# A fused convolution, attention and expert kernel: the group 1/sqrt of the convolution seeded by a GpSimd power

## The reference, cut to what matters

```python
def _gn(v, G=32, eps=1e-05):
    B_, H_, W_, C_ = v.shape
    g = v.reshape(B_, H_, W_, G, C_ // G)
    m = jnp.mean(g, axis=(1, 2, 4), keepdims=True)
    s = jnp.var(g, axis=(1, 2, 4), keepdims=True)
    return ((g - m) / jnp.sqrt(s + eps)).reshape(v.shape)

x = x + _L0_conv_ref(_gn(x), L0_conv_W1, L0_conv_b1)
```

## Time and profile before

| what | value |
| --- | --- |
| three runs | 760.74, 761.24, 767.37 us; median 761.24 |
| the profiled execution | 759.72 us |
| its span, first to last instruction | 757.9 us |
| granted TensorE clock, mean over the span | 0.974 of full speed |
| busy over the span | PE 91%, PEld 82%, DVE 61%, ACT 44%, POOL 34% |

### The profile page before, as it was taken

One profiled execution on the slowest core, in us unless ns is written; L12 is line 12 of the kernel. 1 busy time (PEld: TensorE's weight loads), 2 busy tenths in 40 slices (PEclk: granted clock), 3 DMA queues, 4 the chain that ended last, 5 costly groups with the idle time before them and its releaser, 6 DMA issues.

```text
span 757.9 us, 16610 instructions
## 1 busy us (share of the span) xinstructions
PE 691.6 (91%) x4136; PEld 619.3 (82%) x4137; DVE 465.8 (61%) x1718; ACT 335.1 (44%) x500; POOL 259.9 (34%) x250
## 2 busy tenths in 40 slices
PE   3987886899999999994799999999999999999993
PEld 3876776788878788882699999998999998999893
DVE  5788988667777787777445454454545444454541
ACT  2433334566666667561343443433344343333330
POOL 3544554105343443434232232322223232322322
PEclk9999999999999999997799999999999999999997
DMA  8211111002121211112622222222222222222221
GB/s 270 87 47 47 31 49 42 12 11 80 47 73 52 68 57 44 72 43 89 179 36 37 42 31 42 36 37 36 37 41 32 42 36 37 36 37 41 32 31 16
DMA packets 32570, 40.08 MB, mean 53 GB/s; under 512 B 4853, under 2 KB 27990, under 8 KB 32424
## 3 DMA queue, kind: packets, MB, share of 16 engines
q1 hardware_dynamic: 18566, 25.98, 12.0%
q0 software_dynamic: 13296, 13.35, 11.6%
q10 hardware_dynamic: 690, 0.55, 0.3%
HBM read 22.38 MB, written 17.47 MB: 53 GB/s over the span
## 4 chain that ended last, share of the span: by engine, by line
DMA 33%; issue 10%; DVE 5%; PE 1%; SPq 1%; DVEq 1%; POOLq 0%; POOL 0%; ACT 0%
DMA out_rows<-y_sb,y_id 32%; DVE y_sb L1017 3%; DVE y_id L1014 1%; PE ps L1034 1%; DVE y_sb L1012 1%; DMA slot_rows<-lists 1%; DVEq L1012 1%; SPq L424 0%; POOLq L606 0%; DVEq L1017 0%; SPq L425 0%; SPq L486 0%; POOL out_rows L603 0%; SPq L487 0%; SPq L497 0%
## 5 line engine op out<-in xcount | busy, mean ns | idle before, releaser
L603 POOL DMA_INDIRECT out_rows<-y_sb,y_id x71 | 110.8, 1560 | 273.4 <-DVE y_sb L1017 260.0
L1034 PE MATMUL ps<-w_o_sb,hT 128*128 x852 | 158.2, 336 | 10.1 <-DVE hT L1022 6.1
L1034 PEld LDWEIGHTS ps<-w_o_sb,hT 128*128 128x128 f32 x852 | 137.7, 191 | 26.8 <-issue 26.8
L700 ACT ACTIVATE h_sb<-ps 128x768 f32<-128x768 f32 x71 | 57.5, 810 | 224.0 <-PE ps L1034 224.0
L1012 DVE TENSOR_TENSOR y_sb<-ps,b_o_sb 128x192 f32<-128x192 f32 x71 | 25.4, 358 | 170.8 <-DMA out_rows<-y_sb,y_id 165.2
L1034 PE MATMUL ps<-w_hi,sT_hi 96*128 (+1 forms) x284 | 103.8, 365 | 1.3 <-DVE sT_lo L1000 1.3
L1034 PE MATMUL ps<-w_hi,sT_lo 96*128 (+1 forms) x284 | 97.5, 343 | 0.0
L1034 PE MATMUL ps<-w_lo,sT_hi 96*128 (+1 forms) x284 | 97.0, 342 | 0.0
L700 ACT ACT_TABLE_LOAD x71 | 91.1, 1283 | 6.4 <-issue 5.1
L1022 DVE COPY hT<-ps 128x384 f32<-128x384 f32 x142 | 72.1, 550 | 1.4 <-PE ps L1236 1.4
L1236 PE MATMUL ps<-const,h_sb 128*128 128x128 f32 x426 | 58.2, 273 | 1.9 <-ACT h_sb L700 1.9
(11 more groups left out here) (192 smaller groups left out, 1308.8 us busy)
## 6 DMA issues: line engine op xcount, KB each, us to landing
slot_rows<-lists SPq DMA_DIRECT2D x71, 97.0 KB, 2.1
w_o_sb<-in_w_o SPq DMA_DIRECT2D x8, 576.0 KB
out_rows<-w_o_sb SPq DMA_DIRECT2D x16, 192.0 KB, 1.8
h_sb<-in_split_w SPq DMA_DIRECT2D x9, 288.0 KB
hT<-in_split_w SPq DMA_DIRECT2D x9, 288.0 KB
w_o_sb<-in_x SPq DMA_DIRECT2D x1, 1536.0 KB, 12.3
out_rows<-y_sb,y_id POOLq DMA_INDIRECT x71, 3.5
w_o_sb<-in_x SPq DMA_DIRECT2D x1, 768.0 KB, 9.0
```

Of the source, the lines that this page charges most:

```text
L603: pool.indirect_dma_start(out=out, out_offset=bass.IndirectOffsetOnAxis(ap=y_id[:, 0:1], axis=0), in_=y_sb[:, :], in_offset=None, compute_ ...
L700: act.activation(h_sb[:, :].rearrange("p (b n) -> p b n", b=2), ps_h, ACT.Gelu).then_inc(h_done, 1)
L1034: return pe.matmul(dst, lhsT, rhs, start=start, stop=stop)
```

## The change

The seed no longer comes from bit arithmetic on DVE but from a power on GpSimd, gvar to the -0.5, with a tile of constants -0.5 as its second operand. One Newton round is left of three. GpSimd's order in a step becomes xc, power, w_lo, xn. DVE's order in the middle of the step becomes: gneg, gvar, both bn_stats, gsum reduction, first multiply (it waits for the power), bn_aggr, second multiply, copy of the moments, grs, gsq reduction. So the gsq reduction stands behind grs, where it stood ahead of the third round before.

```diff
+        minus_half = sb("minus_half", [P, GROUPS])
+        gpow = sb("gpow", [P, GROUPS])
...
+        gvar_done, gpow_done = sem("gvar_done"), sem("gpow_done")
...
+                         (minus_half[:, :], -0.5))
...
+                if not absent(i + 2):
+
+                    wait(pool, grs_done, i + 2)
+                    wait_alone(pool, gvar_done, i + 3, ld_const)
+                    pool.tensor_tensor(gpow[:, :], gvar[:, :], minus_half[:, :], ALU.pow).then_inc(gpow_done, 1)
                 if not absent(i + 1, NSLICE):
...
                     dve.wait_ge(gsq_done, i + 3)
+                    wait(dve, gpow_done, i + 2)
                     dve.tensor_scalar(gneg[:, :], ps_gsq, -0.5 * INV_GROUP, -0.5 * LN_EPS, ALU.mult, ALU.add)
-                    chain.link(dve.tensor_scalar(gvar[:, :], ps_gsq, INV_GROUP, LN_EPS, ALU.mult, ALU.add))
-                    wait(dve, xn_done, i + 2)
-                    chain.mark(dve.tensor_scalar(grs[:, :].bitcast(i32), gvar[:, :].bitcast(i32), -0.5,
-                                                 float(0x5F3759DF), ALU.mult, ALU.add))
+                    dve.tensor_scalar(gvar[:, :], ps_gsq, INV_GROUP, LN_EPS, ALU.mult, ALU.add).then_inc(gvar_done, 1)
                 if not absent(i - 1):
                     wait_alone(dve, conv_read, i, ld_const)
-                    dve.bn_stats(stats[:, 0, :], X[:, ds((i - 1) * HALVES, 1), :])
-                if not absent(i + 2):
-                    chain.wait()
-                    chain.mark(dve.tensor_tensor(newton[:, :], gneg[:, :], grs[:, :], ALU.mult))
-                if not absent(i - 1):
-                    dve.bn_stats(stats[:, 1, :], X[:, ds((i - 1) * HALVES + 1, 1), :])
-                if not absent(i + 2):
-                    chain.wait()
-                    chain.mark(dve.tensor_tensor(newton[:, :], newton[:, :], grs[:, :], ALU.mult))
+                    for t in range(HALVES):
+                        dve.bn_stats(stats[:, t, :], X[:, ds((i - 1) * HALVES + t, 1), :])
...
                 if not absent(i + 2):
-                    chain.wait()
-                    chain.mark(dve.scalar_tensor_tensor(grs[:, :], newton[:, :], 1.5, grs[:, :], ALU.add, ALU.mult))
+                    wait_alone(dve, gpow_done, i + 3, ld_const)
+                    chain.mark(dve.tensor_tensor(newton[:, :], gneg[:, :], gpow[:, :], ALU.mult))
...
-                    chain.mark(dve.tensor_tensor(newton[:, :], gneg[:, :], grs[:, :], ALU.mult))
+                    chain.mark(dve.tensor_tensor(newton[:, :], newton[:, :], gpow[:, :], ALU.mult))
...
                 if not absent(i + 2):
                     chain.wait()
-                    chain.link(dve.tensor_tensor(newton[:, :], newton[:, :], grs[:, :], ALU.mult))
-                    chain.mark(dve.scalar_tensor_tensor(grs[:, :], newton[:, :], 1.5, grs[:, :], ALU.add, ALU.mult))
+                    wait(dve, xn_done, i + 2)
+                    dve.scalar_tensor_tensor(grs[:, :], newton[:, :], 1.5, gpow[:, :], ALU.add,
+                                             ALU.mult).then_inc(grs_done, 1)
+                elif not absent(i - 1):
+                    chain.wait()
                 if not absent(i + 3):
                     dve.wait_ge(sq_done, i + 4)
                     wait(dve, gsq_done, i + 3)
                     dve.tensor_reduce(gsq[:, :], grouped(xsq[:, :, :]).rearrange("p t g c -> p g t c"),
                                       AX.XY, ALU.add).then_inc(gsq_in, 1)
-                if not absent(i + 2):
-                    chain.wait()
-                    chain.link(dve.tensor_tensor(newton[:, :], gneg[:, :], grs[:, :], ALU.mult))
-                    chain.link(dve.tensor_tensor(newton[:, :], newton[:, :], grs[:, :], ALU.mult))
-                    dve.scalar_tensor_tensor(grs[:, :], newton[:, :], 1.5, grs[:, :], ALU.add,
-                                             ALU.mult).then_inc(grs_done, 1)
-                elif not absent(i - 1):
-                    chain.wait()
...
-            pipeline(dve, conv_or_scales, **CONV, chain=chain, per=12)
+            pipeline(dve, conv_or_scales, **CONV, chain=chain, per=4)
```

More of the change, by code:

```diff
@@ L523, in _ @@
                          (sT_hi[KC:KC + 1, NKC - 1, :].bitcast(f32), 1.0),
-                         (sT_lo[KC:KC + 1, NKC - 1, :].bitcast(f32), 0.0))
+                         (sT_lo[KC:KC + 1, NKC - 1, :].bitcast(f32), 0.0),
+                         (minus_half[:, :], -0.5))
             for n, (dst, value) in enumerate(last_rows):
```

## The result

The changed kernel takes 815.42 us (median of 4 executions, 813.15 to 820.96) against 761.68 (760.74 to 767.37): a ratio of 1.070 with a 95% interval of 1.062 to 1.078. It is slower by about 54 us; 748 had been forecast, within 740 to 774.

A forecast was written before the change was run, and what follows sets the result against it. The prediction took the convolution's ring of grs, xn, xc and statistics as the bound; gains of 10.9 + 0.7 + 1.2 + 0.6 = 13.4 us gave 746.3 for the profiled execution, 748 as median, range 740 to 774.

The forecast's parts named there:

- The bound: In the convolution, grs, xn, xc and the next statistics form a ring of 7.09 us a turn; savings there reach the end.
- The cause of the 1.9 us of stall: Small DVE instructions in the convolution stand still while a GpSimd instruction runs, 1.9 us a turn.
- The ring 5.1 + p: A convolution turn after the change takes 5.1 us plus p, the power's duration; 6.1 us at p = 1.0.
- the break-even at p = 2.0: The change gains while the power in each convolution turn takes under 2.0 us, and loses beyond that.
- That the multiply loses to w_lo: DVE's first multiply after the power starts behind w_lo's start and ends 0.06 us behind w_lo, which takes 1.8 us.
- The price of the power: The GpSimd power over 128x32 in each convolution turn takes p = 1.0 us, with ends of 0.25 and 3.0.
- The law of the steps: The GpSimd power takes 0.2 us plus, per element, some ten plain steps of 2.2 ns; thirty would give 2.3 us.
- the prediction's own sum: Gains over the convolution's eleven turns, the two behind, the start and the next turn: 13.4 us at p = 1.0.
- A: Rival: the power in the convolution ring is slow, 3.0 us, costing 16.1 us more, 777 us; chance 0.24.
- PE as the floor: In the convolution, PE's own work keeps a turn from falling below 5.5 to 6.0 us.
- rival D: The first power, at the start, costs once: some 5 us later by the skill's page, 753 us; chance 0.04.

The follow-up runs named there:

- mult: The changed kernel with a multiply on GpSimd in place of the power, so grs is not the 1/sqrt: 739.57 us, ratio 0.969 to the kernel before.
- seed_dve: The changed kernel's order with the bit-trick seed on DVE, one Newton round and no power: 736.09 us, ratio 0.970 to the kernel before.
- newton_psum: The kernel before with gvar, gneg and the Newton product in PSUM, all three rounds kept: 739.20 us, ratio 0.968.
- idle_power: The kernel before with an added GpSimd power over constants behind each xn, its result read by nobody: 798.95 us, ratio 1.052.
- after_psum: The changed kernel with gneg and the Newton product in PSUM: 803.09 us, ratio 1.052 to the kernel before.
- pow4: The changed kernel with the power over 4 of 32 columns, the others held constant: 746.50 us, ratio 0.977 to the kernel before.

## Why the prediction was wrong

**The bound** held. The ring of grs, xn, xc and statistics set the turn before and after. What was won or lost by the last xn came out in the time: 53.6 and 53.2 us in the changed kernel. In the other profiled executions, against their chips' median before, the two agree within 2 us in five of seven; mult's time is 4 us better than its last xn, that of seed_dve 4 us worse.

**The cause of the 1.9 us of stall** held for w_lo: newton_psum took it away by moving operands alone. Its general form, that small DVE instructions stand still while a GpSimd instruction runs, was too wide: they don't during a power (0.17 us in idle_power), and a multiply that takes one operand from PSUM doesn't beside w_lo (0.18 to 0.20 us). This had no part in the miss.

**The ring 5.1 + p** held over the whole range, with p as measured: 5.35 for 0.25, 6.12 for 1.01, 8.02 for 2.90, 10.52 for 5.43. So did the break-even at p = 2.0: the runs at 1.01 and 2.90 lie 16.9 us below and 16.9 above their kernels before (13.6 and 14.3 by the last xn), with the middle at 1.95, which is ten columns.

**That the multiply loses to w_lo** held: 1711 ns in the changed kernel, 0.20 us where it read from PSUM.

**The price of the power failed.** This is the term that was mis-sized: "I take p = 1.0, near xn's 0.86, as estimate, and keep 0.25 and 3.0 as ends." It is 5.43. The law of the steps was of the right form, a fixed part and a part per element, and its fixed part was not far off: 0.2 assumed, 0.38 measured. But 0.158 us an element is 72 times the 2.2 ns of a plain one, where the estimate had ten and went up to thirty. The wrong end was worse than the wrong middle. The upper end of 3.0 rested on w_lo's 1.81 us and on a guess of thirty steps, and neither says anything on a power: a long plain instruction bounds no other operation. Put with p = 5.43, the prediction's own sum gives 11 x 3.44 = 37.8 us for the turns, 10.5 + 9.4 - 12.2 = 7.7 for the two behind, 3.2 and 3.8 for the start: 52.5 where the last xn is 53.6 later. That is closer than the sum was right: it left out the turn from 18.68 to 26.18, 7.50 us before and 9.60 after, 2.1 more, and the start and the turn behind it grew by 2.9 and 3.4 in place of 3.2 and 3.8 (the first two xn are at 15.34 and 24.94). The rival whose mechanism came true is A, with 0.24; its 777 us, at p = 3.0, is as short as p was.

**PE as the floor** was put at 5.5 to 6.0. It is at most 5.3, as seed_dve's turns of 5.29 show, with PE busy throughout. The prediction itself said that its 5.96 held tails of waits; how much of the difference they are was not traced. The floor would have mattered only for a cheap power.

**A first call's cost** (rival D) didn't show: the first power took 5.47 us and the next 5.43, and it started at 8.98, right behind the end of xc at 8.92, so that no gap hides ahead of it. The Trainium skill, "GPSIMD Engine Reference", section 2.1, tells of about 6 us at the first call of a freshly loaded kernel; no run here shows such a call for the power.

**The page on elementwise work** that was weighed in the prediction ("GPSIMD Engine Reference", section 3.1, of the Trainium skill: about 2.6 cycles an element with two inputs) fits plain operations and not the power. At 1.2 GHz its figure is about 2.2 ns an element, an estimate. From the multiply over 32 elements (0.25 us) to w_lo's 768 (1.81 us) GpSimd takes 2.1 ns more for each, and from 4 to 32 elements the power takes 158 ns more for each.

## What to carry to other kernels

Before work is moved to an idle engine, measure that operation at that size there: its price can't be read from the plain operations around it, and where the ring has 2 us to give, an unknown of 5 decides alone. When the range of an unmeasured price is set, an upper end must come from something that contains the operation; without it the range has to stay wide on that side. A trial over 4 and 16 elements, as here, would have shown the slope. And when small DVE instructions last several times their usual length, look at what GpSimd runs at that moment. Moving the variance, minus its half and the Newton product to PSUM gave 24 us here and left nothing out, about as much as the 22 us of dropping two Newton rounds.

## What the runs showed of the hardware

- GpSimd's power over 128 partitions: 1.01 us for 4 elements a partition, 2.90 for 16, 5.43 for 32, with variances and with constants alike; a multiply over the same 32 takes 0.25.
- Not every GpSimd instruction makes DVE stand throughout. w_lo does (1.81 us, multiply 1711 ns); the power doesn't, though it reads two operands from SBUF: DVE's multiplies with two SBUF operands ran in 0.17 us inside it. The Trainium skill, "SBUF — State Buffer", section "SBUF: two separate sides", has the shared pair of ports held for the whole of a GpSimd instruction. The trace agrees for w_lo and differs for the power, and the trace decides. Why DVE runs beside the power was not tried.
- A DVE tensor_tensor or scalar_tensor_tensor that reads one operand from PSUM and one from SBUF runs beside w_lo in 0.18 to 0.20 us. Two forms stand behind it with one input from SBUF and an SBUF output: a copy of four elements (0.77 us in after_psum) and the integer seed (1.61 us in seed_dve; beside xc, with its input in PSUM, it takes 0.19 in newton_psum). Why these stand was not tried.
- PE's granted clock fell to 0.82 of full speed over the eleven turns of the changed kernel, where PE is busy 78.68 of 115.74 us, from 0.98 at 65.53 of 78.03. These are means over its two levels, 1.2 and 2.4 GHz. It cost no time there: the turns are 5.1 + p as in pow4, where the clock is 1.00, and the two turns behind, at 0.66, take 19.80 us where the ring with p = 5.43 sums to 19.96.
